# Two head groups in one bank of attention outputs, the head mask in the output weights, the residual by ScalarE and GpSimd

## The reference

```python
x = x + attn(layernorm(x)); x = x + ffn(layernorm(x))
# attn: 16 heads of 8 numbers, 512 x 512 scores per head
q, k, v = (y @ W.T + bias).reshape(b, s, 16, 8)
attn = softmax(q k^T / sqrt(8)) * head_mask[None, :, None, None]
out  = (attn @ v).reshape(b, s, 128) @ Wo.T + bo
# ffn: a shared expert plus the 2 best of 8 routed experts, weighted by the two probabilities
shared + sum over the chosen e of gate_e * (gelu(y @ Wfc[e] + bfc[e]) @ Wproj[e] + bproj[e])
```

## Time and profile before

| | |
|---|---|
| median of three executions | 700.1 us |
| profiled execution, time | 700.0 us |
| profiled execution, span from first to last instruction | 698.2 us |
| granted TensorE clock, mean | 0.975 of 2.4 GHz |
| busy: PE matmuls, DVE, ACT, POOL | 633.9, 540.3, 437.9, 256.6 us |

### The profile page before, as it was taken

How to read it: one execution, slowest core, us unless ns; L and a number is a source line. 1 busy time by engine, 2 the same in 40 slices (tenths; PEclk the granted TensorE clock), 3 DMA queues, 4 the chain that set the end, 5 groups by cost and what they waited for, 6 DMA issues and landing times.

```text
span 698.2 us, 13370 instructions
## 1 busy us (share of the span) xinstructions
PE 633.9 (91%) x3934; PEld 324.6 (46%) x3976; DVE 540.3 (77%) x1180; ACT 437.9 (63%) x953; POOL 256.6 (37%) x386
## 2 busy tenths in 40 slices
PE   1766799999999999999999999997979999999996
PEld 1441222323323323323332332323779999998965
DVE  6998778888998998988989989822656666666558
ACT  0881467777687787787787787793425555555541
POOL 6766200020430420421521512506464555454541
PEclk9996799999999999999999999999999999999998
DMA  5399594411311212212221121000112222212174
GB/s 151 93 335 349 126 237 107 115 46 36 92 44 43 83 43 68 69 45 63 63 64 48 58 69 48 21 1 31 47 50 66 66 65 63 68 59 62 47 246 127
DMA packets 67611, 61.28 MB, mean 88 GB/s; under 512 B 16250, under 2 KB 58106, under 8 KB 67562
## 3 DMA queue, kind: packets, MB, share of 16 engines
q1 hardware_dynamic: 63242, 51.79, 26.7%
q0 software_dynamic: 4320, 8.89, 3.8%
HBM read 35.76 MB, written 24.62 MB: 86 GB/s over the span
## 4 chain that ended last, share of the span: by engine, by line
PE 63%; DVE 14%; issue 7%; SPq 5%; POOL 4%; ACT 4%; DMA 3%; DVEq 0%; ACTq 0%; POOLq 0%; another core or an unknown queue 0%
PE ps L1183 13%; PE ps L1172 13%; PE ps L1154 12%; PE ps L1357 10%; PE ps L1369 8%; DVE mx L827 6%; POOL slots L514 2%; DVE x_sb L1097 2%; SPq L295 2%; DMA q_op<-mxT 2%; PE ps L1309 1%; DVE o_t L835 1%; PE ps L1209 1%; PE ps L1317 1%; SPq L305 1%
## 5 line engine op out<-in xcount | busy, mean ns | idle before, releaser
L676 ACT ACTIVATE probs<-ps 128x512 f32<-128x512 f32 x512 | 278.8, 595 | 102.5 <-PE ps L1172 87.8
L827 DVE TENSOR_REDUCE mx<-ps 128x2 f32<-128x1024 f32 x256 | 304.0, 1212 | 42.8 <-PE ps L1154 37.5
L1154 PE MATMUL ps<-k_op,q_op 96*128 96x512 bf16 x512 | 181.5, 394 | 19.2 <-DVE mx L827 7.0
L1172 PE MATMUL ps<-q_op,k_op 128*128 128x512 bf16 x470 | 179.0, 387 | 2.2 <-DMA q_op<-mxT 1.5
L1172 PEld LDWEIGHTS ps<-q_op,k_op 128*128 128x128 bf16 x512 | 49.6, 98 | 187.5 <-ACT probs L676 127.7
L1183 PE MATMUL ps<-probs,v_op 128*32 128x512 f32 x1024 | 136.0, 604 | 0.5 <-issue 0.2
L723 ACT ACTIVATE probs<-ps,b_cur 128x128 f32<-128x128 f32 x284 | 81.4, 368 | 75.7 <-PE ps L1357 65.3
L577 POOL DMA_INDIRECT results<-rest,row_id x71 | 73.9, 1041 | 75.1 <-DVE rest L1041 57.1
L514 POOL DMA_INDIRECT slots<-route_sb,slot_u x64 | 67.0, 1046 | 75.1 <-ACT probs L676 50.8
L1357 PE MATMUL ps<-xn,qk 128*128 128x128 f32 x568 | 79.2, 284 | 3.7 <-DVE xn L1034 1.7
L1154 PEld LDWEIGHTS ps<-k_op,q_op 96*128 96x128 bf16 x512 | 49.5, 99 | 61.7 <-DVE mx L827 27.6
(11 more groups left out here) (135 smaller groups left out, 591.8 us busy)
## 6 DMA issues: line engine op xcount, KB each, us to landing
q_op<-q_scr SPq DMA_DIRECT2D x96, 96.0 KB
k_op<-k_scr SPq DMA_DIRECT2D x96, 96.0 KB
w_sb<-in_W SPq DMA_DIRECT2D x18, 256.0 KB, 4.0
probs<-slots SPq DMA_DIRECT2D x71, 64.5 KB, 1.9
k_scr<-probs SPq DMA_DIRECT2D x16, 256.0 KB, 3.7
q_scr<-probs SPq DMA_DIRECT2D x8, 384.0 KB, 3.1
k_scr<-probs SPq DMA_DIRECT2D x8, 384.0 KB, 3.6
k_scr<-probs SPq DMA_DIRECT2D x16, 128.0 KB, 3.1
```

The costliest lines, as they stand in the source:

```text
L676: nc.scalar.activation(probs[:, i, j, :], ps[:, BK_S + j % key_banks(b, hg), :], ACT.Exp, scale=float(D) ** -0.5).then_inc(s_exp, 1)
L827: nc.vector.reduce_max(mx[:, slot % 2, 2 * p:2 * p + 2], ps[:, bank:bank + 2, :], AX.X).then_inc(s_max, 1)
L1154: last = nc.tensor.matmul(ps[:, BK_A + a % 4, :], q_op[hg][0:SH, j, P * i:P * (i + 1)], k_op[hg][0:SH, j, :], start=True, stop=True)
L1172: nc.tensor.matmul(ps[:, BK_S + j % key_banks(b, hg), :], k_op[hg][:, j, P * i:P * (i + 1)], q_op[hg][:, j, :], start=True, stop=True).the ...
```

## The change

- **Two groups, one bank.** The values of an odd group stand in columns 16 to 24 of `v_op` instead of 0 to 8. Its matmuls add to the bank that the even group before it began (start flag only with an even group's first key tile, stop flag only with an odd group's last). `out_norm` runs once for two groups: in groups 2 and 0. A transpose, a reciprocal of 32 numbers and a multiplication of 256 per partition take the place of two of 512, 16 and 128 each.
- **Mask.** It arrives as one value per row of `wo_sb`, and POOL multiplies it into `wo_sb` once. Three of SP's early DMAs go.
- **Residual.** ACT copies the projection from PSUM to `projected` after the exponential of group 1, step 5 (`AP_STEP` = -11), and POOL adds it to x between its seventh and eighth scatter. `max_rows` for group 2 waits for ACT's copy. For the last sequence DVE still does it.
- **Moved.** `ln2_stats` from p = 3 to p = 6; `Y_STEPS` to 3, 6, 9, 12; `transpose_y` from step 13 to 14 and so `copy_yT` from 15 to group 3's step 0; `router` from step 1 to 3; router steps from p = 1, 2, 4, 5 to 2, 3, 4, 5; `gather_v(b, 3)` ahead of `ln2_scales`.
- **Counts.** `run_bf` += `seq_n` goes from DVE to POOL's end of a sequence, for all sequences but the last.

```diff
-        Y_STEPS = (-1, 3, 7, 11)
+        PV_LAG, MX_STEP, YT_STEP = 11, 7, 14
+        Y_STEPS = (3, 6, 9, 12)
+        AP_STEP = -11
+        ROUTER_STEP, ROUTER_PAIRS = 3, (2, 3, 4, 5)
...
-            nc.gpsimd.memset(v_op[:, :, :, :, 0:1], 1.0).then_inc(s_pad, 1)
+            for hg in range(HG):
+                nc.gpsimd.memset(v_op[:, hg, :, :, HALF_OUT * (hg % 2):HALF_OUT * (hg % 2) + 1], 1.0).then_inc(s_pad, 1)
...
+            def residual(b):
+                if b == 0:
+                    pool.wait_ge(s_xbo, B)
+                pool.wait_ge(s_apc, b + 1)
+                sl = x_sb[:, b * NT:(b + 1) * NT, :]
+                nc.gpsimd.tensor_tensor(sl, sl, projected[:, :].rearrange("p (n c) -> p n c", c=C), ALU.add).then_inc(s_x2, 1)
+            def count_rows(b):
+                pool.wait_ge(s_cn, (b + 1) * Q + 1)
+                pool.wait_ge(s_rk, b + 1)
+                nc.gpsimd.tensor_tensor(run_bf[:, :], run_bf[:, :], seq_n[:, :], ALU.add).then_inc(s_cn, 1)
...
+            nc.gpsimd.tensor_scalar(wo_sb[:, :], wo_sb[:, :], mask_sb[:, 0:1], None, ALU.mult).then_inc(s_wom, 1)
...
+                    if n == NC - 1 and b > 0:
+                        residual(b - 1)
                     if b > 1:
                         route_step(b, n)
+                gather_v(b, 3)
                 if b > 0:
                     ln2_scales(b - 1)
-                gather_v(b, 3)
...
+            def copy_projection(b):
+                act.wait_ge(s_ap, b + 1)
+                wait(act, s_x2, b)
+                nc.scalar.activation(projected[:, :], ps[:, BK_M, :], ACT.Copy).then_inc(s_apc, 1)
...
+                            if step == AP_STEP and not first:
+                                copy_projection(b - 1)
...
-                        if 3 <= p < 7 and hg > 0:
-                            out_norm(b, hg - 1, p - 3)
-                        elif 3 <= p < 7 and not first:
-                            out_norm(b - 1, HG - 1, p - 3)
+                        if 3 <= p < 7 and hg == 2:
+                            out_norm(b, 0, p - 3)
+                        elif 3 <= p < 7 and hg == 0 and not first:
+                            out_norm(b - 1, 1, p - 3)
                         if not first:
                             if hg == 1:
-                                if p == 1:
-                                    residual(b - 1)
-                                if p == 3:
+                                if p == 6:
                                     ln2_stats(b - 1)
...
-                                            start=(i == 0), stop=(i == NT - 1))
+                                            start=(hg % 2 == 0 and i == 0), stop=(hg % 2 == 1 and i == NT - 1))
...
                 if hg == 2:
-                    wait(pe, s_x2, b)
+                    wait(pe, s_apc, b)
...
-                            if hg == 3 and s == 1:
+                            if hg == 3 and s == ROUTER_STEP:
                                 router(b - 1)
```

More of the change, by code:

```diff
@@ L80, in block_kernel @@
         bv_sb, bo_sb = sb("bv_sb", [P, C]), sb("bo_sb", [P, C])
-        mask_sb = sb("mask_sb", [P, HG])
+        mask_sb = sb("mask_sb", [P, 1])
         w1_sb, b1_sb = sb("w1_sb", [P, NE, F]), sb("b1_sb", [P, NE, FC])
@@ L110, in block_kernel @@
         o_t = sb("o_t", [P, S // 32, 32])
-        o_rec = sb("o_rec", [P, S // 32])
+        o_rec = sb("o_rec", [P, S // 32, 2])
         o_all = sb("o_all", [P, S // 32, HG, D])
@@ L140, in block_kernel @@
         yT_now = xnT[:, 0, :]
+        projected = rest[:, 0, 0, :]
         parts = probs.rearrange("p i j s -> p (i j s)").bitcast(bf16)[:, 0:DEEP * 2 * PARTS * S]
@@ L170, in block_kernel @@
         ps = ctx.enter_context(nc.psum_tensor("ps", [P, 8, 512], f32))
-        s_w1st = sem("first_weights_loaded")
+        s_w1st, s_wom = sem("first_weights_loaded"), sem("wo_masked")
+        s_apc = sem("projection_copied")
         s_wo, s_x, s_w, s_wffn = sem("wo_loaded"), [sem("x_loaded0"), sem("x_loaded1")], sem("weights_loaded"), sem("ffn_weights_loaded")
@@ L222, in sequences @@
                 body(b)
-        N_W1ST, N_W = 6, 8
+        N_W1ST, N_W = 6, 5
         TILE_PARTS = (slice(0, 2 * NT), slice(2 * NT, B * NT))
@@ L249, in block_kernel @@
         L2 = 9
-        N_PAD = 6
+        N_PAD = 5 + HG
+        HALF_OUT = 16
         N_PADS, N_TAB = 2, N_MAT + 13
@@ L273, in _ @@
             sp.dma_start(iota_sb[:, :], iota8).then_inc(s_w, 16)
[L274 to L277, removed]
+            sp.dma_start(mask_sb[:, :], head_mask.rearrange("(c o) -> c o", o=1)).then_inc(s_w, 16)
             sp.dma_start(wr_sb[:, :], Wr).then_inc(s_w, 16)
@@ L519, in _ @@
             max_split(0)
+            pool.wait_ge(s_wo, 16 * J)
+            pool.wait_ge(s_w, 16 * N_W)
+            nc.gpsimd.tensor_scalar(wo_sb[:, :], wo_sb[:, :], mask_sb[:, 0:1], None, ALU.mult).then_inc(s_wom, 1)
             pool.wait_ge(s_xn, B)
@@ L557, in gather_and_route @@
                     keep_yT(b - 1)
+                    count_rows(b - 1)
             sequences(gather_and_route)
@@ L827, in row_max, with out_norm @@
                 nc.vector.reduce_max(mx[:, slot % 2, 2 * p:2 * p + 2], ps[:, bank:bank + 2, :], AX.X).then_inc(s_max, 1)
-            def out_norm(b, hg, step):
-                g = b * HG + hg
+            def out_norm(b, pair, step):
+                n = b * (HG // 2) + pair
+                both = o_t[:, :, :].rearrange("p a (h c) -> p a h c", h=2)
                 if step == 0:
-                    wait(dve, s_onrm, g)
-                    dve.wait_ge(s_pv, (g + 1) * NT)
+                    wait(dve, s_onrm, n)
+                    dve.wait_ge(s_pv, (n + 1) * 2 * NT)
                     nc.vector.transpose(o_t[:, :, :].rearrange("p a c -> p (a c)"), ps[:, BK_O, :]).then_inc(s_ot, 1)
                 elif step == 1:
-                    dve.wait_ge(s_ot, g + 1)
-                    nc.vector.reciprocal(o_rec[:, :], o_t[:, :, 0]).then_inc(s_orec, 1)
+                    dve.wait_ge(s_ot, n + 1)
+                    nc.vector.reciprocal(o_rec[:, :, :], both[:, :, :, 0]).then_inc(s_orec, 1)
                 elif step == 2:
-                    dve.wait_ge(s_orec, g + 1)
-                    if hg == 0:
+                    dve.wait_ge(s_orec, n + 1)
+                    if pair == 0:
                         wait(dve, s_o, b)
[L843 to L848, removed]
+                    nc.vector.tensor_tensor(o_all[:, :, 2 * pair:2 * pair + 2, :], both[:, :, :, 1:1 + D],
+                                            o_rec[:, :, :].unsqueeze(3).to_broadcast([P, S // 32, 2, D]),
+                                            ALU.mult).then_inc(s_onrm, 1)
+                elif pair == 1:
+                    dve.wait_ge(s_onrm, n + 1)
                     wait(dve, s_ap, b)
@@ L852, in residual @@
             def residual(b):
-                if isinstance(b, int) and b == 0:
-                    dve.wait_ge(s_xbo, B)
+                dve.wait_ge(s_xbo, B)
                 dve.wait_ge(s_ap, b + 1)
-                sl = x_sb[:, bass.ds(b * NT, NT), :]
+                sl = x_sb[:, b * NT:(b + 1) * NT, :]
                 nc.vector.tensor_tensor(sl, ps[:, BK_M, :].rearrange("p (n c) -> p n c", c=C), sl, ALU.add).then_inc(s_x2, 1)
@@ L907, in count_step @@
                     dve.wait_ge(s_rt, (b + 1) * R)
+                    dve.wait_ge(s_cn, (b + 1) * Q)
                     nc.vector.reduce_sum(seq_n[:, :], chosen[:, :, :].rearrange("p c e -> p e c"), AX.X).then_inc(s_cn, 1)
@@ L956, in _ @@
             for step in range(4):
-                out_norm(B - 1, HG - 1, step)
+                out_norm(B - 1, 1, step)
             residual(B - 1)
@@ L1179, in pv @@
                 if i == 0:
-                    wait(pe, s_ot, g)
+                    if hg % 2 == 0:
+                        wait(pe, s_ot, g // 2)
                     pe.wait_ge(s_vop, g + 1)
@@ L1202, in project_out @@
                 if i == 0:
-                    pe.wait_ge(s_wo, 16 * J)
+                    pe.wait_ge(s_wom, 1)
                     pe.wait_ge(s_o, b + 1)
```

10 lines of the change are left out of this document (4 added, 6 removed).

## The result

The changed kernel takes 714.6 us (median of four executions, 713.59 to 715.07), the kernel before on the same chip 700.7. The ratio is 1.0197, 95% interval 1.0175 to 1.022: 13.8 us slower, by the ratio, or 713.9 us from the 700.1 that the forecast started from. The profiled execution took 715.07 us with a span of 713.2, 15.0 more than the 698.2 before.

What follows compares the result with a forecast made beforehand. The prediction took a chain of key scores, exponential, key scores with two banks to set the pace. Six sequences at +1.28, sequence 7's +1.3 and +0.4 once gave +9.4 on 700.1: 709.5 us, range 702.5 to 714.5.

Steps and rivals of the forecast that it cites:

- the copy: Group 1's c1: PE's max_rows waits for ACT's copy of the projection, +0.40 us per sequence, bounds 0 and 0.60.
- DVE's lateness in group 1: Group 1's c3: PE's wait for late maxima goes without out_norm and residual, -0.33 us per sequence.
- the scales: Group 2's c0: later statistics make ACT's y wait for POOL's scales, +0.76 us per sequence, bounds 0 and 1.15.
- y after step 12: Group 2's c3: y delays the second exponential and step 3's key scores, +0.17 us per sequence, bounds 0 and 0.43.
- copy_yT and router: Group 3's c0: copy delays the second exponential, router stands behind pv, +0.68 us per sequence, bounds 0.2 and 0.95.
- the moved router steps: Group 3: the step moved to p = 2 could fill DVE's gap, giving c3's gain its lower bound of 0.
- the gain in group 3's c3: PE's wait for the maxima ends earlier as out_norm goes, -0.40 us per sequence, bounds 0 and 0.69.
- The last sequence: Sequence 7: group 1 +0.07, scales wait about +1.2, moved copies cancel, DVE idle: +1.3 us.
- Once only: Three more memsets on POOL +0.3 and the last sequence's longer out_norm +0.1: +0.4 us in all.
- the insertions are hidden: Rival: ACT's spare time holds the moved work and the DVE stalls go; 695.4 us, chance 0.08.
- DVE as the bound: Rival: DVE bounds the kernel, 2.1 us less in each of seven sequences, -14.7; 685.4 us, chance 0.02.
- the DVE stalls stay: Rival: the stalls only move, so the gains in groups 1 and 3 are lost; 714.6 us, chance 0.07.

Runs made afterwards that it cites:

- stats3: Changed kernel with the layer norm's statistics back at pair 3 of group 1 instead of pair 6: 708.56 us, ratio 1.0129 to the kernel before.
- bank: Kernel before with only the shared bank, one normalisation for two groups and the mask in the output weights; nothing moved or offloaded: 695.85 us, ratio 0.9932.
- yback: Changed kernel with y at steps 3, 6, 9, 11, its transposes, copy, router and router steps back at earlier places: 704.92 us, ratio 1.0058.
- ap12: Changed kernel with ScalarE's copy of the projection one exponential earlier, after step 4 of group 1: one execution of 706.41 us on a faster chip.
- pair1: Changed kernel with DVE's copy of the logits at pair 1 of group 3 and the step after it at pair 2: 710.91 us, ratio 1.0146.
- ranks13: bank with router steps at pairs 1, 2, 3, 4 and the ranks in step 13 of group 3: 684.37 us on a faster chip, ratio 0.9925.
- bank2: Kernel of bank run once more, on the chip of ranks13b: 696.60 us, ratio 0.9928 to the kernel before.
- ranks13b: Kernel of ranks13 run once more, beside the kernel before and bank2 on one chip: 693.21 us, ratio 0.9891 to the kernel before.
- both: Changed kernel with the edits of stats3 and yback together: 689.96 us on a faster chip, ratio 1.0002 to the kernel before.

## Why the prediction was right or wrong

**The direction and most terms held; the size was 4 to 5 us short.** 709.5 was said, and 714.6 measured beside a kernel before of 700.7; by the ratio that is 713.9 from the 700.1 of the forecast. This is 0.6 inside the range's upper end of 714.5 and above the 713.5 of the forecast itself. +9.4 was the sum and +13.8 came. That the range still holds it is in part luck: the term that the forecast lacked (4.2) was made up in part by a sequence 0 shorter by 1.2 and by once-only costs that did not come. What was written as a loss for one sequence, term by term: the copy +0.40 (0.35), DVE's lateness in group 1 -0.33 (-0.31), the scales +0.76 (0.79), y after step 12 +0.17 (0.15), copy_yT and router +0.68 (0.68), y after steps 6 and 9 0 (0: the mean of 3.03 in group 2's c1 is one cycle of 3.25 in sequence 2, with the late exponential told under both, and 2.98 in the others). Each of these comes from one chain read in one cycle, key scores, exponential, key scores, and stats3, bank, yback and ap12 confirmed them, except that the parts of copy_yT and router weren't separated.

**The step that failed** is the moved router steps. The prediction said that "the router step that moved from p = 1 to 2 fills the gap" on DVE, and looked only at what DVE would be late for. It never asked who waits for that step: PE's transpose of the maxima for the next sequence, in step 7, waits until the logits are out of BK_M. At pair 2 the copy stands behind that pair's maxima, and ends at 273.68, 0.8 after PE has issued step 7's key scores. +0.70, six times, 4.2 us; pair1 takes exactly that back in the cycles.

**A mis-sized term**: the gain in group 3's c3 was 0.24 instead of 0.40. PE's wait for the maxima ended at 279.07, T + 1.16 (T = 277.91), where T + 1.0 was said. It is still there, so DVE is still late in this cycle; ranks13, with the ranks and router steps moved, took another 0.30.

**The last sequence**: +1.3 said, +1.9 measured (0.03 in groups 0 and 1, 2.05 in group 2, -0.14 in group 3). Group 2's c0 grew by 1.31 (3.73 against 2.42), where about 1.2 was said, but c3 grew by 0.75 (3.40 against 2.65). "The moved copies cancel" was wrong: PE's transposes now wait for y there too.

```profile
473.75 0.66 PE L1251 MATMUL ps<-id_sb,route_sb 128*128 128x128 f32 x4 [1.05 <-ACT route_sb L667]
```

yback gave 0.75 back in c3, and took 0.49 in c2.

**Once only**: +0.4 said, about 0 measured. The first exponential came 0.37 earlier, not 0.3 later; four memsets took 0.27 together. Sequence 0 was 1.20 shorter, which I don't count as the change's: 1.0 of it is c3 of its group 1, whose end waits for rows that a DMA brings (q_op from mxT), and which takes from 2.94 to 4.67 in the profiles of the experiments, 3.67 and 4.27 in bank and bank2, the same kernel. Behind the attention are the 1.63 of the clock.

The sum of the profile: -0.4 (start) - 1.2 (sequence 0) + 12.8 (sequences 1 to 6 and groups 0 and 1 of 7) + 2.05 (group 2 of 7) - 0.14 (group 3) + 1.9 (behind) = 15.0.

**The rivals.** That the insertions are hidden needed a c0 of group 3 under 3.65; it is 4.33. For DVE as the bound the condition was a saturated VectorE (the rule is that of the Trainium skill, Perfetto Trace Analysis, "Optimizing Scalar/DVE Operations"). The trace stands against the condition: DVE lost 17 us of work over the execution (540.3 to 523.4), spent 31 us more waiting for PE, and the time rose. The scales were not in time. The rival in which the DVE stalls stay had the price of 714.6 us, the number that was measured, but not by its mechanism: the stall of group 1 went, and that of group 3 shrank by 0.24.

## What to carry to other kernels

Relief for a busy engine is worth only the waits that others have for it: in the run bank 11.8 us less of DVE's work were worth 3.6 us by the cycles and 4.8 by the ratio. Before an instruction is moved, find the chain that sets the cycle and ask at which point of a cycle the engine has time, since 0.98 us of spare time were none behind the first exponential. And for each step moved later, list who waits for it, above all through a shared bank: the dearest term missed was one small copy behind another instruction of its own queue.

## What the runs showed of the hardware

- A reciprocal on DVE of 32 numbers per partition took 0.34 us (after), against 0.24 for 16 (before): one for both groups saves 0.14 of two.
- GpSimd's residual of 128x512 took 1.28 us in the mean (after) beside DVE's maxima from PSUM, as long as its adds of the same size before the attention (1.26).
- The same kernel takes 3.57 or 5.20 us for the same 32 matmuls, with a granted clock of 1.00 or 0.68 in them (ranks13b, ranks13). In the 3.5 us ahead of them PE was busy 1.8 us in the first case and 0.7 in the second; but stats3, with 0.7 too, has 1.00. What decides it wasn't found.
- The same kernel before took 700.4 us on one chip and 689.5 on another, so only ratios on one chip compare. The difference isn't in the attention: ranks13 (faster chip) and ranks13b are one kernel with 8.8 us between the medians, and their cycles in the attention agree within 0.01 us from sequence 1 on. From the last exponential to the end they took 217.96 and 226.80 us, 8.8 apart. The other two profiles on the faster chip (both, ap12) have 216.6 and 219.1 there, those on other chips 226.5 to 228.9.
